# Second attention: the output product without its identity and bias products

## Chip, core and metric

One core of a Trainium2 chip runs the whole program. The metric is the time on the device in microseconds, smaller is better. The three runs of the kernel before took 1669.58, 1671.32 and 1675.81 us, median 1671.32.

## The reference

Two transformer layers over 4096 tokens of width 256. Each layer adds attention and a feed-forward part to its input. The change is in the second layer's attention, a gated linear attention by chunks of 128 tokens:

```python
xn = _layernorm(x, axis=-1)
x = x + _L1_attn_ref(xn, ...) + _L1_ffn_ref(xn, ...)

# in _L1_attn_ref: M is the state of a head, 32 x 32
M = M * f_t[..., None, None] + g_t[..., None, None] * scale * (k_t[..., :, None] * v_t[..., None, :])
y_t = jnp.einsum('bhd,bhde->bhe', q_t, M) * o_t[..., None]
...
return jnp.einsum('bld,ed->ble', y, Wout) + bout
```

So every row of the result is x + y Wout^T + bout, and the second feed-forward part, a mixture of eight experts of which each token takes two, is added to that later.

## The kernel before

The program runs in stages: the first attention and routing (to about 400 us), the first experts, then from about 790 us the rest of the first layer's sums with the norms for the second layer (the shared stage), the second attention (880 to 1130 us), and the second experts, which take the rest. All steps of the middle part stand in one list, `plan2`. Every engine walks through it and does its own share of each step; semaphores tie the engines together, and each engine keeps the list's order. The list is written by hand: `BEHIND` puts steps behind the products of the shared stage, `TURN` and `LATE` are the order of one turn of the second attention, and `AMONG` puts single steps between.

The activations lie in SBUF in `ACC`, 32 chunks of 128 tokens by 256. The second attention takes one chunk a turn, 32 turns, in the order `ORDER1` (all eight batches' first chunks, then the second ones). One turn n holds, on TensorE in this order: the value product (`project_val`, line 1753) for chunk n; the query and key product (`project_qk`, line 1741) for chunk n+1; transposes of queries and keys (`turn`, lines 1769 and 1777); the state products and the sums of chunk n-1 (`keys`, `update`, lines 1813, 1822, 1827); sixteen affinity products of chunk n (line 1795); and the output product of chunk n-1 (`project_out`, lines 1836 to 1840).

The output product accumulates in one PSUM region: the identity times the chunk's rows of `ACC` (this adds x), two products with Wout, and a bf16 product of three rows of ones with the bias split in three bf16 parts (`ones3`, `BO3`). ScalarE then copies the region over the chunk's rows in `ACC` (line 1344) and signals `oe_put`.

The other engines in a turn:
- VectorE: state update (line 2353, turns 8 to 23), the decay scan (`decay`, line 2334, 128x1024, both operands in SBUF), rotary products (lines 2314, 2325, 2326), and the weighing of the affinities (`affinity`, line 2341), which signals `w_put`. `project_val` of the next turn waits for `w_put`, since affinities and values share a PSUM bank.
- ScalarE: value scalings (line 1303), copies of the transposes (1310, 1315), of the sums (1321), key scalings (1339), the output copy (1344).
- GpSimd: opening (`open_gates`, lines 1030 and 1036: the gated queries of chunk n+1, on which the transposes of the next turn wait), and in turns 6 to 29 two or three indirect DMAs that scatter routing rows (line 929), in a pattern of three, three, two. In the shared stage it adds sums of 128x1024 (`sums`, line 1001, and `combine`, line 1011), and at one place it splits the bias (`bias_split`).
- SyncE: loads the decays of each turn (line 802), weights of the second experts (788, 848) and stores finished rows, eight chunks at a time (`store_sums`), when `oe_put` has counted them. Before the second experts TensorE waits for all 32 of `oe_put`.

Of the kernel before, what the change touches and what calls it, by code (L numbers as in the profile page):

```python
# [92 lines left out]
def attention_order():  # L93
# [10 lines left out]
    for idx in range(-LEAD, NH + 7):  # L104
# [83 lines left out]
        ("open", 1), ("decay_load", 2)]  # L188
# [43 lines left out]
def second_order():  # L232
# [19 lines left out]
    out += [("rows",)] + [(kind, NT - 1) for kind in ("update", "sums_copy", "project_out", "out_copy")]  # L252
# [47 lines left out]
def build(nc, t, out):  # L300
    ctx = ExitStack()
    with ctx:
# [140 lines left out]
        BO3 = view(carve(128), 128, BF16)  # L443
        ones3 = view(carve(64), 64, BF16)
# [20 lines left out]
        NB1 = view(small + 186, 32)  # L465
        assert pt_at + 2560 + 2048 <= LIMIT - 7680
# [98 lines left out]
        stk_set, v_set = sem("stk_set"), sem("v_set")  # L565
# [11 lines left out]
        b_in, b_cut, b_rows, b_set = sem("b_in"), sem("b_cut"), sem("b_rows"), sem("b_set")  # L577
# [10 lines left out]
        none_set, slot_in, slot_turned, slot_off, slot_put = (sem(n) for n in ("none_set", "slot_in", "slot_turned", "slot_off", "slot_put"))  # L588
# [27 lines left out]
        out_made, oe_put, sums_out = (sem(n) for n in ("out_made", "oe_put", "sums_out"))  # L616
# [28 lines left out]
        def sync(sp):  # L645
# [50 lines left out]
            def maxrow(n):  # L696
                bk, use = banks0["maxrow", n]
                sp.wait_ge(bank[bk], use + 1)
                sp.wait_ge(s_made, 24 * n + 24)
                sp.wait_ge(stk_set, 3)  # L700
# [9 lines left out]
            def clear(p):  # L710
                sp.wait_ge(cst_in, 32)
                sp.wait_ge(none_set, 4)
# [41 lines left out]
            sp.wait_ge(b_cut, 5)  # L754
            sp.wait_ge(b_set, 1)
# [118 lines left out]
        def gpsimd(pool):  # L874
# [5 lines left out]
            for v in Vb:  # L880
                pool.memset(v, 0.0).then_inc(v_set)
            pool.wait_ge(v_set, 2)
            for v in Vb:
                pool.memset(v[:, :, :, 16:17], 1.0).then_inc(v_set)
            pool.wait_ge(v_set, 4)
            for n in range(3):
                if n:
                    pool.wait_ge(stk_set, n)
                pool.memset(STK[n][1][96:99, :, :].rearrange("p j s -> p (j s)").bitcast(F32), ONES2).then_inc(stk_set)
            pool.wait_ge(stk_set, 3)  # L890

            def clear_meta():
                for n, apart in enumerate((128, 0)):
                    pool.memset(unused[n][0:NTILE, :, :], 0.0).then_inc(none_set)
                    pool.wait_ge(none_set, 2 * n + 1)
                    pool.iota(unused[n][0:NTILE, :, 1], [[1, 128]], base=T, channel_multiplier=apart, allow_small_or_imprecise_dtypes=True).then_inc(none_set)
                pool.wait_ge(none_set, 4)
# [11 lines left out]
            def bias_rows():  # L909
                pool.memset(B2S, 0.0).then_inc(b_set)  # L910
                pool.wait_ge(b_in, 32)
                for k in range(3):
                    if k:
                        pool.wait_ge(b_cut, 2 * k)
                    pool.tensor_copy(b3[0:8, k, :], bstage[0:8, :]).then_inc(b_cut)
                    if k < 2:
                        pool.wait_ge(b_cut, 2 * k + 1)
# [120 lines left out]
            def bias_split():  # L1038

                pool.wait_ge(const1_set, 2)  # L1040
                pool.memset(ones3, 0.0).then_inc(const1_set)
                for k in range(3):
                    pool.wait_ge(const1_set, 3 + k)
                    pool.memset(ones3[32 * k:32 * k + 1, :], 1.0).then_inc(const1_set)
                pool.wait_ge(const1_set, 6)
                pool.tensor_copy(BO3, BO).then_inc(const1_set)
                pool.wait_ge(const1_set, 7)
                pool.tensor_tensor(BO, BO, BO3, ALU.subtract).then_inc(const1_set)
                for k in (1, 2):
                    pool.wait_ge(const1_set, 7 + k)  # L1050
                    pool.tensor_copy(BO3[32 * k:32 * k + 32, :], BO[32 * k:32 * k + 32, :]).then_inc(const1_set)
                pool.wait_ge(const1_set, 10)
                pool.tensor_tensor(BO[64:96, :], BO[64:96, :], BO3[64:96, :], ALU.subtract).then_inc(const1_set)
                pool.wait_ge(const1_set, 11)
                pool.tensor_copy(BO3[64:96, :], BO[64:96, :]).then_inc(const1_set)
                pool.wait_ge(const1_set, 12)

            for kind, *a in plan2:
# [6 lines left out]
                elif kind == "const1":  # L1065
                    const1()
                    bias_split()
# [14 lines left out]
        def scalar(act):  # L1082
# [44 lines left out]
            def project_v(b, half):  # L1127
                bk, use = banks0["project_v", b, half]
                act.wait_ge(v_made, 2 * b + half + 1)
                act.wait_ge(v_set, 4)  # L1130
# [255 lines left out]
        def tensor(pe):  # L1386
# [1085 lines left out]
```

## Time and profile before

| | us |
|---|---|
| span of the profiled execution | 1669.4 |
| median of three runs | 1671.32 |
| PE busy | 1569.7 (94%) |
| PE weight loads busy | 1210.1 (72%) |
| DVE busy | 823.6 (49%) |
| ACT busy | 734.2 (44%) |
| POOL busy | 714.7 (43%) |

PE is TensorE, PEld its weight loads, DVE VectorE, ACT ScalarE, POOL GpSimd and SP SyncE. The times are of one execution that the profiler recorded. The chain that ended last is PE for 79% of the span, DVE for 9%, DMA for 4%. The identity product (line 1836) has 32 calls and the bias product (line 1840) too; a float32 product shows as two matmuls. The rows further down are lines of a timeline or of a table of windows. A busy matmul row can hide waits, since matmuls are pipelined and their ends are modelled; the start of an instruction is what the semaphores let through.

### The profile page before, as it was taken

Reading aid. Unit: us, or ns where it says so; the run is one execution under the profiler, and the core shown is the slowest. Engines: PE = TensorE matmul, PEld = TensorE weight load, DVE = VectorE, ACT = ScalarE, POOL = GpSimd, SP = SyncE. Lnnn points to the kernel's source line nnn. Section 1 sums busy time; section 2 is a strip of 40 time slices with the busy share of each in tenths; the row PEclk is TensorE's granted clock in tenths of the full one; section 3 lists DMA queues with packets and bytes.
Section 4 is the critical chain, followed back from the end, with each engine's and each line's share of the span. In section 5 each row is a group of like instructions: output and inputs, shape, how many; then the busy total and the mean of one; then the engine's idle time right before and its main releaser. Section 6 shows DMA issues by size and latency. Waiting matters only on the chain.

```text
span 1669.4 us, 32480 instructions
## 1 busy us (share of the span) xinstructions
PE 1569.7 (94%) x11054; PEld 1210.1 (72%) x11054; DVE 823.6 (49%) x2298; ACT 734.2 (44%) x1923; POOL 714.7 (43%) x815
## 2 busy tenths in 40 slices
PE   6989989999999999999997799988999999999997
PEld 3545445555548999998664567768999999999996
DVE  6867898787812223221477788873221122222220
ACT  4544545555541222222566466644333233333332
POOL 3122336666523555553810467752333333333332
PEclk9989999999999999999999999999999999999999
DMA  8534325534305222222621396466222222222221
GB/s 269 131 103 110 79 70 105 106 91 103 67 17 230 73 70 72 72 70 88 216 103 65 102 221 99 78 123 259 33 38 39 33 39 39 34 37 39 34 38 23
DMA packets 86093, 151.07 MB, mean 90 GB/s; under 512 B 16276, under 2 KB 64272, under 8 KB 82864
## 3 DMA queue, kind: packets, MB, share of 16 engines
q1 hardware_dynamic: 61392, 111.62, 25.3%
q0 software_dynamic: 24544, 37.38, 10.3%
q8 instruction: 96, 1.57, 0.4%
q14 instruction: 61, 0.50, 0.1%
HBM read 104.10 MB, written 44.45 MB: 89 GB/s over the span
## 4 chain that ended last, share of the span: by engine, by line
PE 79%; DVE 9%; DMA 4%; issue 3%; ACT 3%; SPq 1%; POOL 0%; another core or an unknown queue 0%; DVEq 0%; ACTq 0%; POOLq 0%
PE PS L1634 23%; PE PS L1652 22%; PE PS L1491 4%; PE PS L1427 3%; DVE PS L1954 3%; PE PS L1741 3%; PE PS L1476 3%; PE PS L1455 2%; PE PS L1608 2%; PE PS L1562 2%; PE PS L1619 2%; PE PS L1517 2%; PE PS L1437 2%; PE PS L1753 1%; DMA arena<-FD 1%
## 5 line engine op out<-in xcount | busy, mean ns | idle before, releaser
L1634 PEld LDWEIGHTS PS<-arena 128*128 128x128 f32 x3408 | 396.6, 192 | 15.8 <-DVE arena L2174 4.6
L1634 PE MATMUL PS<-arena 128*128 128x128 f32 x3408 | 403.8, 275 | 3.2 <-DVE arena L2174 3.2
L1652 PE MATMUL PS<-arena 128*128 x1704 | 392.4, 379 | 0.0
L1652 PEld LDWEIGHTS PS<-arena 128*128 128x128 f32 x1704 | 311.7, 190 | 40.2 <-issue 0.2
L2174 DVE COPY arena<-PS 128x256 f32<-128x256 f32 x142 | 60.3, 425 | 414.8 <-PE PS L1619 404.2
L1954 DVE CUSTOM_DVE_ANT_0 PS<-PS,arena 128x512 f32<-128x512 f32 (+3 forms) x512 | 235.5, 523 | 46.1 <-PE PS L1455 42.4
L970 POOL DMA_INDIRECT out<-arena x71 | 111.8, 1574 | 313.1 <-ACT arena L1246 292.4
L1236 ACT ACTIVATE arena<-PS,arena 128x128 f32<-128x128 f32 x568 | 162.3, 369 | 137.6 <-PE PS L1634 137.5
L1246 ACT ACTIVATE arena<-PS,arena 128x256 f32<-128x256 f32 x142 | 67.4, 474 | 283.1 <-PE PS L1654 191.3
L903 POOL TENSOR_SCALAR_AFFINE_SELECT arena<-arena 128x256 f32<-128x256 f32 x256 | 100.0, 414 | 207.9 <-ACT arena L1152 207.5
L1152 ACT ACTIVATE arena<-PS 128x512 f32<-128x512 f32 (+1 forms) x256 | 166.3, 704 | 49.9 <-PE PS L1476 40.3
L956 POOL DMA_INDIRECT arena<-XN,arena x142 | 144.4, 1017 | 93.8 <-PE PS L1619 51.9
L929 POOL DMA_INDIRECT SLOT<-arena x128 | 156.1, 1220 | 30.2 <-issue 30.2
L2186 DVE COPY arena<-arena 128x1024 f32 (+1 forms) x142 | 136.7, 963 | 61.7 <-ACT arena L1228 57.9
L963 POOL DMA_INDIRECT SUM<-arena x71 | 70.3, 990 | 111.6 <-ACT arena L1246 105.0
L1455 PE MATMUL PS<-arena 96*128 96x512 bf16 (+3 forms) x512 | 99.8, 307 | 6.0 <-DVE arena L1954 5.8
L1476 PE MATMUL PS<-arena 99*128 99x512 bf16 (+3 forms) x512 | 98.0, 308 | 5.7 <-ACT arena L1152 4.8
L1228 ACT ACTIVATE arena<-PS 128x512 f32<-128x512 f32 x71 | 42.4, 597 | 113.9 <-PE PS L1634 108.4
L1476 PEld LDWEIGHTS PS<-arena 99*128 99x128 bf16 x512 | 45.6, 99 | 57.8 <-issue 20.2
L1455 PEld LDWEIGHTS PS<-arena 96*128 96x128 bf16 x512 | 49.2, 99 | 46.6 <-DVE arena L1954 16.3
L1491 PE MATMUL PS<-arena 128*32 128x512 f32 (+3 forms) x1024 | 75.7, 435 | 4.5 <-DVE arena L1940 3.6
L2334 DVE TENSOR_TENSOR_SCAN arena<-arena 128x1024 f32<-128x1024 f32 x32 | 73.1, 2286 | 7.6 <-DMA arena<-FD 7.5
(246 smaller groups left out, 1985.6 us busy)
## 6 DMA issues: line engine op xcount, KB each, us to landing
arena<-FD SPq DMA_DIRECT2D x32, 512.0 KB
arena<-in_w SPq DMA_DIRECT2D x16, 1024.0 KB
SPL<-arena SPq DMA_DIRECT2D x32, 384.0 KB, 2.6
arena<-SPL SPq DMA_DIRECT2D x64, 192.0 KB
XN<-arena SPq DMA_DIRECT2D x16, 512.0 KB, 3.2
arena<-SPL SPq DMA_DIRECT2D x64, 128.0 KB
arena<-SUM SPq DMA_DIRECT2D x16, 512.0 KB, 6.4
arena<-in_x SPq DMA_DIRECT2D x8, 512.0 KB, 6.4
```

The lines of the kernel that those rows point to most:

```text
L929: pool.indirect_dma_start(SLOT[layer], bass.IndirectOffsetOnAxis(ap=POS[:, n, i:i + 1], axis=0), META[:, i, n, :], None).then_inc(row_out[ ...
L956: pool.indirect_dma_start(MOE[layer].xr[i % 4][:, :], None, XN, row).then_inc(tile_in[i % 4], 16)
L970: pool.indirect_dma_start(out, row, m.y[i % 3][:, :], None, compute_op=ALU.add).then_inc(y_out[i % 3], 16)
L1152: act.activation(PB[h % NPB][:, lo:hi], ps(3, lo, hi), ACT.Exp, scale=0.25).then_inc(p_made)
L1236: ins = act.activation(m.hT[i % len(m.hT)][:, 128 * f:128 * f + 128], ps(m.UPB[i % 2], 128 * f, 128 * f + 128), ACT.Gelu, bias=m.bias[i % ...
L1455: ins = pe.matmul(ps(0, o, o + w), q[0:96, j, 128 * i:128 * i + 128], k[0:96, j, 0:w], start=True, stop=True)
L1476: ins = pe.matmul(ps(3, o, o + w), k[0:99, j, 128 * kb:128 * kb + 128], q[0:99, j, 128 * kb:512], start=True, stop=True)
L1491: ins = pe.matmul(PS[32 * j:32 * j + 32, 6, 128 * kb:512], vb[:, kb, 8 * half + jj, :], PB[(8 * n + jj) % NPB][:, OFFT[kb]:OFFT[kb] + w], ...
L1634: ins = pe.matmul(o, m.now[i % 2][:, c * F + 128 * f:c * F + 128 * f + 128], m.xt[i % 2][:, 128 * c:128 * c + 128], start=(c == 0), stop=( ...
L1652: ins = pe.matmul(to, m.hT[i % len(m.hT)][:, 128 * c:128 * c + 128], m.WD[:, bass.ds(e * (nf * 256) + c * 256, 256)], start=(c == 0), stop ...
L1954: dve.tensor_tensor_reduce(sc, sc, MASK[:, 384 - 128 * r:512], -1.0, -NEG, ALU.add, ALU.min, NM[n % 2][:, r, j:j + 1]).then_inc(s_max)
L2186: dve.tensor_copy(m.now[i % 2][:, :], m.WU[:, bass.ds(e * m.wrow, m.wrow)]).then_inc(w_staged)
```

## The change

TensorE's output product has only its two products with Wout. ScalarE copies them from PSUM into a single SBUF buffer `OUT1` (over constants that are not read any more) and signals `out_put`. GpSimd adds `OUT1` to the chunk's rows of `ACC` (`out_add`, 128x256) and signals `oe_put`; the step stands behind `open` in a turn, for chunk n-1. ScalarE's copy of chunk n waits for the addition of chunk n-1. The bias is added to `ACC` earlier, 128x1024 for each of the eight batches (`bias_add`), once the second layer's norm of the batch has read them; GpSimd does it at the list's step `xa`. The bias split and its constants are gone, and some semaphores are merged (`stk_set`, `v_set`, `none_set`, `b_set`).

```diff
 TURN = [...
         ("sums_copy", -1), ("project_out", -1), ("keys", 0), ("weigh", 0), ("out_copy", -1), ("rope_add", 1),
-        ("open", 1), ("decay_load", 2)]
+        ("open", 1), ("out_add", -1), ("decay_load", 2)]
...
+        OUT1 = NONE[:, 0:256]
...
-            def bias_split():
...
+            def bias_add(b):
+                pool.wait_ge(xn_made, b + 1)
+                four = ACC[:, 4 * b:4 * b + 4, :]
+                pool.tensor_tensor(four, four, BO.unsqueeze(1).to_broadcast([128, 4, 256]), ALU.add).then_inc(bo_put)
+
+            def out_add(n):
+                i = ORDER1[n]
+                pool.wait_ge(bo_put, min(n + 1, NB))
+                pool.wait_ge(out_put, n + 1)
+                pool.tensor_tensor(ACC[:, i, :], ACC[:, i, :], OUT1, ALU.add).then_inc(oe_put)
...
             def project_out(n):
                 act.wait_ge(out_made, n + 1)
-                act.activation(ACC[:, ORDER1[n], :], ps(1, 256, 512), ACT.Copy).then_inc(oe_put)
+                if n:
+                    act.wait_ge(oe_put, n)
+                act.activation(OUT1, ps(1, 256, 512), ACT.Copy).then_inc(out_put)
...
             def project_out(n):
 
                 if n:
-                    pe.wait_ge(oe_put, n)
-                else:
-                    pe.wait_ge(const1_set, 12)
-                pe.matmul(ps(1, 256, 512), ident, ACC[:, ORDER1[n], :], start=True, stop=False)
+                    pe.wait_ge(out_put, n)
                 pe.wait_ge(yt_put, n + 1)
                 for g in range(2):
-                    pe.matmul(ps(1, 256, 512), YT[:, 128 * g:128 * g + 128], WOUT[:, g, :], start=False, stop=False)
-                pe.matmul(ps(1, 256, 512), ones3[0:96, :], BO3[0:96, :], start=False, stop=True).then_inc(out_made)
+                    ins = pe.matmul(ps(1, 256, 512), YT[:, 128 * g:128 * g + 128], WOUT[:, g, :], start=(g == 0), stop=(g == 1))
+                ins.then_inc(out_made)
```

## Rows read from the trace of the kernel before

**Rows 1.** Windows: start:end, length, busy us of PE, PEld, DVE, ACT, POOL, clock, DMA.

```profile
998.20:1075.70 77.50, 77.50 (x806) 54.61 (x804) 65.17 (x78) 51.78 (x212) 59.36 (x52) 1.00 0.52 91
```

**Rows 2.** Timeline of one turn: start, duration, engine, line, operation, count, idle before.

```profile
1017.15 0.73 PE L1795 MATMUL PS<-arena 32*128 32x128 f32 x16
1017.80 0.70 PE L1836 MATMUL PS<-arena 128*128 128x256 f32 x2
1017.94 1.22 DVE L2341 TENSOR_TENSOR arena<-PS,arena 128x1024 f32<-128x1024 f32 x1 [0.63 <-PE PS L1795]
1018.34 1.03 PE L1839 MATMUL PS<-arena 128*128 128x256 f32 x4
1019.20 0.27 PE L1840 MATMUL PS<-arena 96*128 96x256 bf16 x1
1019.32 1.10 PE L1753 MATMUL PS<-arena 128*128 128x256 f32 x4
...
1021.97 0.60 PE L1769 MATMUL PS<-arena 128*128 128x128 f32 x4
```

**Rows 3.** Timeline: weighing and next value product in two other turns.

```profile
892.90 1.22 DVE L2341 TENSOR_TENSOR arena<-PS,arena 128x1024 f32<-128x1024 f32 x1 [1.05 <-PE PS L1795]
...
894.59 1.03 PE L1753 MATMUL PS<-arena 128*128 128x256 f32 x4
...
1088.38 1.23 DVE L2341 TENSOR_TENSOR arena<-PS,arena 128x1024 f32<-128x1024 f32 x1 [1.06 <-PE PS L1795]
...
1089.75 1.10 PE L1753 MATMUL PS<-arena 128*128 128x256 f32 x4 [0.55 <-DVE arena L2341]
```

**Rows 4.** Timeline of ScalarE in the turn of rows 2.

```profile
1017.34 0.39 ACT L1321 ACTIVATE arena<-PS 128x256 f32<-128x256 f32 x1 [0.91 <-PE PS L1827]
1017.62 1.79 ACT L1339 ACTIVATE arena<-arena 128x32 f32<-128x32 f32 x8
...
1019.51 0.38 ACT L1344 ACTIVATE arena<-PS 128x256 f32<-128x256 f32 x1
```

**Rows 5.** Timeline of GpSimd in that turn, with VectorE's scan.

```profile
1017.40 0.61 POOL L1030 TENSOR_TENSOR arena<-arena 128x256 f32<-128x256 f32 x1 [0.52 <-DVE arena L2326]
1017.97 0.61 POOL L1036 TENSOR_TENSOR arena<-arena 128x256 f32<-128x256 f32 x1
1018.74 1.00 POOL L929 DMA_INDIRECT SLOT<-arena  x1 [0.16 <-issue]
1019.60 2.28 DVE L2334 TENSOR_TENSOR_SCAN arena<-arena 128x1024 f32<-128x1024 f32 x1
1020.05 2.61 POOL L929 DMA_INDIRECT SLOT<-arena  x1 [0.30 <-issue]
...
1022.96 0.96 POOL L929 DMA_INDIRECT SLOT<-arena  x1 [0.30 <-issue]
```

**Rows 6.** Timeline: a GpSimd product that starts within a scan.

```profile
934.99 2.29 DVE L2334 TENSOR_TENSOR_SCAN arena<-arena 128x1024 f32<-128x1024 f32 x1
935.15 2.53 POOL L1030 TENSOR_TENSOR arena<-arena 128x256 f32<-128x256 f32 x1 [10.36 <-DVE arena L2326]
```

**Rows 7.** Timeline: a small VectorE step beside a GpSimd addition.

```profile
806.08 2.35 POOL L1011 TENSOR_TENSOR arena<-arena 128x1024 f32<-128x1024 f32 x1
...
806.84 1.62 DVE L2231 SCALAR_TENSOR_TENSOR arena<-arena 128x4 f32<-128x4 f32 x1
```

**Rows 8.** Timeline of the shared stage's end, ScalarE and VectorE.

```profile
853.52 2.06 ACT L1288 ACTIVATE arena<-arena 128x256 f32<-128x256 f32 x4
...
863.24 0.29 DVE L2255 COPY arena<-PS 128x128 f32<-128x128 f32 x1 [0.72 <-PE PS L1705]
...
865.83 0.16 DVE L2231 SCALAR_TENSOR_TENSOR arena<-arena 128x4 f32<-128x4 f32 x1
```

**Rows 9.** Timeline of the end of the second attention.

```profile
1129.14 0.95 POOL L956 DMA_INDIRECT arena<-XN,arena  x1 [0.30 <-issue]
...
1130.38 0.41 PE L1619 MATMUL PS<-arena 128*128 128x128 f32 x2 [0.52 <-issue]
```

More of the change, by code:

```diff
@@ L251, in second_order @@
             out.append(("slots",))
-    out += [("rows",)] + [(kind, NT - 1) for kind in ("update", "sums_copy", "project_out", "out_copy")]
+    out += [("rows",)] + [(kind, NT - 1) for kind in ("update", "sums_copy", "project_out", "out_copy", "out_add")]
     return out
@@ L587, in build @@
         r_pos = sem("r_pos")
-        none_set, slot_in, slot_turned, slot_off, slot_put = (sem(n) for n in ("none_set", "slot_in", "slot_turned", "slot_off", "slot_put"))
+        slot_in, slot_turned, slot_off, slot_put = (sem(n) for n in ("slot_in", "slot_turned", "slot_off", "slot_put"))
         row_out = [sem(f"row_out{n}") for n in range(4)]
@@ L615, in build @@
         kd_put, y_made, yt_put, dm_made, m_put = (sem(n) for n in ("kd_put", "y_made", "yt_put", "dm_made", "m_put"))
-        out_made, oe_put, sums_out = (sem(n) for n in ("out_made", "oe_put", "sums_out"))
+        out_made, bo_put, oe_put, sums_out = (sem(n) for n in ("out_made", "bo_put", "oe_put", "sums_out"))
+        out_put = sem("out_put")
         xt_ready = {b: [(banks0[f"xt{c}", b][0], banks0[f"xt{c}", b][1] + 1) for c in range(2)] for b in range(NB)}
@@ L699, in maxrow @@
                 sp.wait_ge(s_made, 24 * n + 24)
-                sp.wait_ge(stk_set, 3)
+                sp.wait_ge(pads_set, 7)
                 if n >= 3:
@@ L711, in clear @@
                 sp.wait_ge(cst_in, 32)
-                sp.wait_ge(none_set, 4)
+                sp.wait_ge(const_set, 7)
                 if p == 0:
@@ L880, in gpsimd @@
             for v in Vb:
-                pool.memset(v, 0.0).then_inc(v_set)
-            pool.wait_ge(v_set, 2)
+                pool.memset(v, 0.0).then_inc(pads_set)
+            pool.wait_ge(pads_set, 2)
             for v in Vb:
-                pool.memset(v[:, :, :, 16:17], 1.0).then_inc(v_set)
-            pool.wait_ge(v_set, 4)
+                pool.memset(v[:, :, :, 16:17], 1.0).then_inc(pads_set)
+            pool.wait_ge(pads_set, 4)
             for n in range(3):
                 if n:
-                    pool.wait_ge(stk_set, n)
-                pool.memset(STK[n][1][96:99, :, :].rearrange("p j s -> p (j s)").bitcast(F32), ONES2).then_inc(stk_set)
-            pool.wait_ge(stk_set, 3)
+                    pool.wait_ge(pads_set, 4 + n)
+                pool.memset(STK[n][1][96:99, :, :].rearrange("p j s -> p (j s)").bitcast(F32), ONES2).then_inc(pads_set)
+            pool.wait_ge(pads_set, 7)
             def clear_meta():
                 for n, apart in enumerate((128, 0)):
[L894 to L897, printed above, removed]
+                    pool.memset(unused[n][0:NTILE, :, :], 0.0).then_inc(const_set)
+                    pool.wait_ge(const_set, 2 * n + 4)
+                    pool.iota(unused[n][0:NTILE, :, 1], [[1, 128]], base=T, channel_multiplier=apart, allow_small_or_imprecise_dtypes=True).then_inc(const_set)
+                pool.wait_ge(const_set, 7)
             def future(h):
@@ L1066, in gpsimd @@
                     const1()
-                    bias_split()
+                elif kind == "xa":
+                    bias_add(*a)
+                elif kind == "out_add":
+                    out_add(*a)
                 elif kind == "gates" and a[1] == 4:
```

34 lines of the change are left out of this document (7 added, 27 removed).

## Prediction

> **What bounds the kernel now.** I read the stretch by windows first, then the timeline of one turn, then the list of waits. The second attention runs 32 turns of about 7.05 us. In the eleven turns from 998.2 to 1075.7 us the matmul row is busy for all 77.50 us, and weight loads for 54.61 [rows 1]. That looks like an engine without a gap, so that any product taken out comes back as time. The timeline of one turn says otherwise. The sixteen affinity products start at 1017.15 and end at 1017.88; VectorE's weighing of them (line 2341) starts at 1017.94. TensorE meanwhile runs the identity, output and bias products (1017.80, 1018.34, 1019.20), and the next turn's first value product (line 1753) starts at 1019.32, 1.38 us after the weighing began [rows 2]. Line 1753 waits for the weighing (project_val, w_put). In a turn where TensorE stood idle, with 0.55 us put down to the weighing, it starts at 1089.75, 1.37 us after a weighing that began at 1088.38 [rows 3]. So the distance in the full turn is the distance of a pure wait. I compared all 31 turns that have a next one: in 27 of them the weight load of line 1753 stands 1.33 to 1.35 us behind the start of the weighing. The two limits coincide: TensorE is through with the three products at 1019.20 + 0.11 = 1019.31, and the wait lets it go on at 1017.94 + 1.37 = 1019.31. The loop that sets the turn is value, query and key products, turns, update, affinity, weighing, and value again. The output product lies beside it, under the weighing.
>
> The Trainium skill (Perfetto Trace Analysis, Identifying the Most-Contended Engine) calls matmul busy share a bad measure of headroom and takes the weight-load share instead. By that measure TensorE has a quarter to spare here (54.61 of 77.50), which speaks against the first rival below.
>
> **The change, part by part.**
>
> 1. TensorE loses the identity product (1018.34 - 1017.80 = 0.54 us up to the next, of which 0.11 is behind the affinity products, so 0.43) and the bias product (1019.31 - 1019.20 = 0.11): 0.54 us a turn [rows 2]. What is late next is the weighing, and it is just as late as before: 0 in 27 turns. The identity product also covered the wait for ScalarE's copy of the sums: that copy runs 1017.34 to 1017.73 [rows 4], and the output products can start at 1017.88, so this wait is over by 0.15 us. If it were not, there are 0.54 us before it would show. In two of the four others something is won. After the weighing of 892.90 the value product starts at 894.59, 1.69 us behind it [rows 3], which is 0.3 more than the wait; a second turn is alike, and the last two wait for routing. I take -0.6 us for the stage, between 0 and -1.
>
> 2. ScalarE's copy has the same size and another target. It starts at 1019.51 now, after the key scalings (1017.62, 1.79 us, so to 1019.41) [rows 4]. The products end 0.54 earlier but the scalings don't, so the copy starts no earlier than about 1019.35 and its result is there at about 1019.8. It now waits for the addition of the row before, a turn back; behind it in ScalarE's queue are the next value scalings. GpSimd would have to be over 6 us late. Cost 0. SyncE's stores of eight rows now wait for GpSimd; behind them are the decay loads, but each store comes more than a turn after its last row. Cost 0, except at the end.
>
> 3. GpSimd gains 32 additions of 128x256, placed behind opening (open). The nearest row is its own 128x256 product at 0.61 us [rows 5]. In a turn with three scatters GpSimd idles for 0.52 us only: opening 1.19, scatters 1.00, 2.61 and 0.96 with their gaps. Of three turns two have three scatters and one has two. The second scatter takes 2.61 instead of 0.96 since VectorE's scan (1019.60, 2.28 us) is running [rows 5]. In the turn at 935.15 a 0.61 us product that starts 0.16 us into a scan takes 2.53 [rows 6]. The addition can't start before 1019.8, so GpSimd stands idle from 1018.58 for 1.2 us and then meets the scan 0.2 us after its start: 2.5 us. In exchange no scatter meets it: -1.65. A turn on time thus costs GpSimd 1.2 + 2.5 - 1.65 = 2.1 us, against 0.52 of idle time, and opening is 1.5 us late in the next. What waits for opening are the transposes, at 1021.97 for a result that is there at 1018.0 [rows 2, 5]: some 3.5 us of slack, so still nothing is lost. In the turn after, the addition's input has long been there and it costs 0.6. I followed this for ten turns. A three-scatter turn needs 1.19 + 0.6 + 0.16 + 1.0 + 2 x (0.30 + 0.96) = 5.5 us unblocked, a two-scatter turn 4.2, and a scan blocks about 2.0 (2.53 - 0.61 = 1.9 for a product, 1.65 for a scatter well inside). Three turns: 15.2 + 6.0 = 21.2 against 3 x 7.05 = 21.15. GpSimd is just full. The slack takes up most of the swing; where opening's second product falls into the scan it ends some 0.2 us after the transposes want it, at worst 0.8, and where GpSimd is first the scan starts up to 0.6 later, which VectorE's idle time mostly takes. For the 24 turns with scatters I take 0.1 us a turn, +2.4, between 0 and +8 (0.33 a turn).
>
> 4. In turns 0 to 5 GpSimd has room, but VectorE is on the path with routing steps that read two SBUF operands. Such an operation waits for a GpSimd addition: line 2231, 0.16 us otherwise, took 1.62 beside a 2.35 us addition [rows 7, 8]. Two of the six additions fall on such steps: +0.8, between 0 and +2.
>
> 5. Eight bias additions of 128x1024, 2.35 us each by the same form [rows 7], 19 us in all, go between GpSimd's sums, where it has gaps; the removed bias split was there too. Their own time costs 0. Their blocking does not: the one for batch 5 waits for a norm that ends at 853.52 + 2.06 = 855.6, and holds up the two-operand step that VectorE has just then (line 2293), with all behind it, by some 2.0 us. VectorE has 0.7 us of idle time before 863.24 [rows 8], from which on it is the chain up to 878. So about +1.3; the one for batch 6 comes on that chain, where it delays a step that now another GpSimd sum delays: about -0.1. +1.2 in all, between -0.5 and +5 (two such collisions in full).
>
> 6. The end. TensorE's last stage waits for the last addition instead of the last copy. GpSimd is gathering until 1130.09, then adds for 0.61, and TensorE, which started at 1130.38, starts at about 1130.9 [rows 9]. The products before end earlier, which doesn't help. +0.5, between 0 and +1.
>
> Sum: -0.6 + 2.4 + 0.8 + 1.2 + 0.5 = +4.3 us. The profiled execution has 1669.4; 1669.4 + 4.3 = 1673.7. The median of the runs is 1671.3, 1.9 above it, so I say 1675.6 for a median.
>
> The rule that speaks against the change is in the Trainium skill (SBUF — State Buffer, Who interferes with whom): a VectorE operation with two SBUF inputs and a GpSimd operation that reads SBUF exclude each other, and whichever started first holds the port for its whole length. The trace agrees [rows 6, 7], though the blocked product took 2.53 and not the 2.12 + 0.61 = 2.73 us that full exclusion gives. With 2.73 each meeting would cost 0.2 more, the three turns 21.8 us, and the sum +5 us or so higher.
>
> **The rivals.**
>
> Faster: TensorE's products set the turn, and the coincidence of the two limits is one of the way matmul ends are modelled. For it: the busy row without a gap. Against it: 1.37 us in turns with idle time, 1.38 in those without. 31 x 0.54 = 16.7 us: 1671.3 - 16.7 = 1654.6.
>
> Slower by GpSimd: it becomes the bound of the turns with scatters. For it: 0.52 us idle against 0.6 of new work, and the addition placed just where the scan starts. It decides once opening ends more than 3.5 us later than now. Then the transposes wait in two of three turns for between 0.2 us and the 1.9 by which a blocked product outlasts a free one, say 1.0: 24 x 2/3 x 1.0 = +16 in place of +2.4, so 1689; with half of that 1681.
>
> Slower in the setup: three bias additions hold VectorE up in full, 3 x 2.35 = +7 instead of +1.2: 1675.6 + 5.8 = 1681. Against it: from 812 to 863 the chain is TensorE's almost alone, and VectorE carries it only from 863.24 on [rows 8].
>
> **How the numbers follow.** Forecast 0.60, faster rival 0.10, GpSimd rival 0.19, setup rival 0.11. The ends of the forecast's terms add up to -1.5 and +16, 1669.8 to 1687.3 for a median; all at one end at once is unlikely, and the runs of before lie 6 us apart, so its own range is 1668 to 1683. With the setup rival and most of the GpSimd one, and a little below for the spread, 1665 to 1688 should hold 8 in 10. The line between same and different is 0.5% (8.4 us), about what a measurement of this kernel can tell from no change: 1663 and 1679.7. Faster: the first rival, 0.10. Slower: most of the GpSimd rival (0.16), a third of the setup rival (0.04) and the forecast's tail (0.02), 0.22. Same: 0.68.
>
> **What would show it.** In the changed kernel line 1753 should still start 1.37 us after the weighing, with about half a microsecond of idle time before it put down to VectorE; the turn should stay at 7.05 to 7.2 us; the additions should show two lengths, about 0.6 and about 2.5 us; GpSimd's idle time in the stretch with scatters should be mostly gone. If turns are 6.5 us the first reason is wrong. If transposes (line 1769) wait for GpSimd by a microsecond or more, the second rival holds.

## The result and the profile after

The changed kernel took 1712.3 us (median of four runs, 1706.5 to 1720.9) where the kernel before took 1670.6 beside it: 1.0239 times as long, 95% interval 1.0215 to 1.0263. The forecast was 1675.6 with a range of 1665 to 1688. It was wrong, by 37 us.

The profiled execution has 1709.3 us, 39.9 more than before. Line numbers of the kernel after are 5 to 8 lower than before (value product 1748, transposes 1764, affinity 1790, sums 1822, output product 1831, weighing 2333, scan 2326, scatters 928, addition 1046). From the timelines I took the start of the first value product, of the seventh (turn 6, where the scatters begin), of the last one, and of the first product of the experts:

| us | before | after | difference |
|---|---|---|---|
| first value product at | 874.75 | 875.92 | +1.2 |
| turns 0 to 5 | 58.95 | 60.89 | +1.9 |
| turns 6 to the last value product | 187.51 | 216.44 | +28.9 |
| from there to the experts' first product | 9.18 | 14.06 | +4.9 |
| from there to the end | 539.05 | 541.96 | +2.9 |

Nearly all is in the 25 turns with scatters. The windows of this stretch, before and then after (columns as in rows 1):

```profile
933.70:1121.21 187.51, 177.97 (x1716) 122.93 (x1716) 144.57 (x162) 109.66 (x445) 128.11 (x114) 0.98 0.64 130
```

```profile
936.82:1153.26 216.44, 181.49 (x1641) 122.19 (x1641) 144.88 (x162) 108.23 (x445) 149.69 (x140) 0.93 0.53 112
```

VectorE and ScalarE do the same work in it (144.9 and 108.2 us busy), and GpSimd's 149.7 is far from 216.4. No engine is full; the turn has become longer by waits. The steady turns were 7.05 us and are now 7.7 to 9.9. One with three scatters, which answers to [rows 2, 4, 5]:

```profile
1027.14 2.28 DVE L2326 TENSOR_TENSOR_SCAN arena<-arena 128x1024 f32<-128x1024 f32 x1
1027.20 0.36 ACT L1339 ACTIVATE arena<-PS 128x256 f32<-128x256 f32 x1
1027.71 2.24 POOL L1046 TENSOR_TENSOR arena<-arena 128x256 f32<-128x256 f32 x1 [1.87 <-ACT arena L1339]
...
1029.51 0.60 PE L1764 MATMUL PS<-arena 128*128 128x128 f32 x4
...
1030.10 1.00 POOL L928 DMA_INDIRECT SLOT<-arena  x1 [0.16 <-PE PS L1764]
...
1031.16 0.64 PE L1822 MATMUL PS<-arena 128*32 128x128 f32 x16
1031.41 0.99 POOL L928 DMA_INDIRECT SLOT<-arena  x1 [0.30 <-issue]
...
1031.73 0.89 PE L1790 MATMUL PS<-arena 32*128 32x128 f32 x15
1032.70 0.96 POOL L928 DMA_INDIRECT SLOT<-arena  x1 [0.30 <-issue]
1032.86 0.36 PE L1790 MATMUL PS<-arena 32*128 32x128 f32 x1 [0.24 <-issue]
...
1034.41 0.38 ACT L1314 ACTIVATE arena<-PS 128x256 f32<-128x256 f32 x1 [3.40 <-remote]
1034.57 1.22 DVE L2333 TENSOR_TENSOR arena<-PS,arena 128x1024 f32<-128x1024 f32 x1 [2.68 <-PE PS L1790]
...
1034.94 1.10 PE L1831 MATMUL PS<-arena 128*128 128x256 f32 x4 [1.72 <-ACT arena L1314]
...
1035.94 0.89 PE L1748 MATMUL PS<-arena 128*128 128x256 f32 x3
```

The value product began at 1026.85, and up to the start of the affinity products all stands where it stood: the transposes 2.66 us in (2.65 in [rows 2]), the sums' products at 4.31. These end at 1031.80 by their record. ScalarE's copy of them (line 1314) should follow 0.1 us later; it starts at 1034.41. The weighing, which waits for the affinity products, starts at 1034.57, and the next value product 1.37 us behind it. The trace also has the events that raise the semaphores: the signal of the sums' products comes 2.59 us after the end of their record. In this stretch the signals of three groups come late, each of them sixteen small products on tiles of 32 rows or columns (keys, sums, affinity); those of value, query and key, and output products and of the transposes come 0.01 to 0.02 us behind, in each turn of this trace, also in the middle of a scatter. (In six of the later traces one or two output products come 0.4 to 2.0 us late too, beside a scatter or gather or right behind late affinity products.) Late signals come where scatters run, and those of the sums and the affinities mostly arrive 0.4 to 0.9 us after a scatter has ended (here the last one ends at 1033.66 and the copy starts 0.75 behind). Before the change the last scatter ended 0.3 us before the sums' products did.

I call these signals late, but TensorE itself is held up too. In each turn of the ten traces below that have no late signals, the last of the sixteen affinity products starts 0.46 us behind the first. Here it starts 1.13 us behind (1031.73 and 1032.86), and 17 of the 32 turns of this trace are stretched in this way, to between 0.6 and 1.35 us.

TensorE's clock adds to it. After such a wait it is granted less for a while. Windows of two turns, the second starting right behind a wait of 2.25 us for the copy:

```profile
1000.73:1009.74 9.01, 6.76 (x71) 4.64 (x71) 5.92 (x8) 4.74 (x21) 6.29 (x6) 1.00 0.75 189
1009.74:1019.08 9.34, 8.94 (x72) 5.70 (x71) 5.93 (x8) 4.95 (x22) 6.25 (x6) 0.82 0.36 64
```

In the second the transposes start 4.35 us into the turn, 1.7 later than usual, and the clock over the turn is a mean of its two levels, 2.4 and 1.2 GHz. Over turns 6 on the clock fell from 0.98 to 0.93: (0.07 x 216.4) - (0.02 x 187.5) = about 11 us of full-speed work not granted, an estimate from above of the clock's share in the 28.9. No run separates the two; a kernel below, with additions that nobody reads, had 0.96 over the same turns and they took 219.1 us.

Read with this in mind, the trace of before has it too, in the few turns where scatters met those products (the affinity products, 0.73 us in [rows 2], take 1.28 here):

```profile
946.22 0.62 PE L1827 MATMUL PS<-arena 128*32 128x128 f32 x16
946.83 1.28 PE L1795 MATMUL PS<-arena 32*128 32x128 f32 x16
946.88 0.97 POOL L929 DMA_INDIRECT SLOT<-arena  x1 [0.30 <-issue]
948.15 0.96 POOL L929 DMA_INDIRECT SLOT<-arena  x1 [0.31 <-issue]
949.92 0.39 ACT L1321 ACTIVATE arena<-PS 128x256 f32<-128x256 f32 x1 [3.15 <-remote]
```

The end of the stage answers to [rows 9]:

```profile
1160.10 1.45 POOL L1046 TENSOR_TENSOR arena<-arena 128x256 f32<-128x256 f32 x1 [7.44 <-ACT arena L1339]
1161.69 1.01 POOL L955 DMA_INDIRECT arena<-XN,arena  x1 [0.15 <-issue]
...
1165.52 0.95 POOL L955 DMA_INDIRECT arena<-XN,arena  x1 [0.30 <-issue]
1166.48 0.73 POOL L1046 TENSOR_TENSOR arena<-arena 128x256 f32<-128x256 f32 x1
...
1167.31 0.66 PE L1614 MATMUL PS<-arena 128*128 128x128 f32 x2 [5.07 <-POOL arena L1046]
```

The gathers stand behind the last but one addition, which waits for ScalarE's copy, and the last addition stands behind four gathers.

### The profile page after: what moved, and what is told of

Read it like the earlier page. It is cut to its first block and busy times, and to the rows that moved or that the text cites. A ratio compares the mean times of both kernels' runs of the same rounds, so it can differ in the third digit from the quotient of the medians.

```text
span 1709.3 us, 32410 instructions
## 1 busy us (share of the span) xinstructions
PE 1575.7 (92%) x10958; PEld 1212.5 (71%) x10958; DVE 827.1 (48%) x2298; ACT 731.8 (43%) x1923; POOL 753.5 (44%) x845
## 5 line engine op out<-in xcount | busy, mean ns | idle before, releaser
L1647 PEld LDWEIGHTS PS<-arena 128*128 128x128 f32 x1704 | 312.1, 190 | 39.9 <-issue 0.2
L928 POOL DMA_INDIRECT SLOT<-arena x128 | 130.3, 1018 | 30.2 <-issue 29.3
```

The source lines that it names most:

```text
L928: pool.indirect_dma_start(SLOT[layer], bass.IndirectOffsetOnAxis(ap=POS[:, n, i:i + 1], axis=0), META[:, i, n, :], None).then_inc(row_out[ ...
L1647: ins = pe.matmul(to, m.hT[i % len(m.hT)][:, 128 * c:128 * c + 128], m.WD[:, bass.ds(e * (nf * 256) + c * 256, 256)], start=(c == 0), stop ...
```

## The experiments

The runs came in five groups, each on one chip with the kernel before beside them. The time of the kernel before differs by group (1664 to 1676), so ratios are to its runs in the same one. "Turns 6 on" is the time from the seventh to the last value product. Whether signals came late turned out to go by group:

- group 1: TensorE's half alone, additions that nobody reads, scatters held, additions behind the scatters: on time;
- group 2: the changed kernel, the kernel before, the gathers first, no scatters: late;
- group 3: the changed kernel, additions that nobody reads, scatters held: late;
- group 4: plain transfers by GpSimd and by SyncE, additions behind the scatters, the kernel before with its scatters later: on time;
- group 5: additions behind the scatters, plain transfers by GpSimd, the changed kernel: late.

A kernel without scatters shows no late signals itself, so for it the group is known from the others.

### TensorE's half alone

```diff
-                pe.matmul(ps(1, 256, 512), ident, ACC[:, ORDER1[n], :], start=True, stop=False)
...
-                pe.matmul(ps(1, 256, 512), ones3[0:96, :], BO3[0:96, :], start=False, stop=True).then_inc(out_made)
+                ins.then_inc(out_made)
```

> The kernel before without the identity and the bias product; ScalarE copies the output products alone, so x and the output bias are left out of the result; nothing is added on GpSimd. The step of the forecast that puts TensorE's 0.54 us a turn under the weighing expects no gain: 1671 +- 2. If TensorE's products set the turn: 1655. Theory C (TensorE) expects the slowdown here: 1700 or more.

1664.9 us, 1.0008 times (0.9985 to 1.0031). Turns of 7.05. The products that go leave an idle time of the kind forecast ahead of the value product; VectorE's weighing, then TensorE:

```profile
1000.46 1.23 DVE L2340 TENSOR_TENSOR arena<-PS,arena 128x1024 f32<-128x1024 f32 x1 [0.63 <-PE PS L1795]
```

```profile
1001.83 1.10 PE L1753 MATMUL PS<-arena 128*128 128x256 f32 x4 [0.38 <-DVE arena L2340]
```

The value product starts 1.37 us behind the weighing, with 0.38 us of waiting put down to it. Removing 0.54 us a turn from TensorE is worth nothing, and it costs nothing.

### GpSimd's half alone, and the scatters' place alone

A copy of the addition in the kernel before, with scratch as its target; and no addition, only the wait.

```diff
-        ("open", 1), ("decay_load", 2)]
+        ("open", 1), ("spare", -1), ("decay_load", 2)]
...
+            def spare(n):
+                if n > NT - 5:
+                    return
+                pool.wait_ge(oe_put, n + 1)
+                if n:
+                    pool.wait_ge(spare_put, n)
+                pool.tensor_tensor(SPARE, SPARE, BO, ALU.add).then_inc(spare_put)
```

```diff
+        ("open", 1), ("hold", -1), ("decay_load", 2)]
...
+                elif kind == "hold":
+                    pool.wait_ge(oe_put, a[0] + 1)
```

> The kernel before, its identity and bias products kept, with 28 more additions of 128x256 on GpSimd, each behind opening and waiting for ScalarE's copy as in the changed kernel; nothing reads their result. Theory A (place): the scatters are pushed as in the changed kernel, turns of 7.6 to 9.9 us, time 1671 + 25 to 35 = 1696 to 1706. Theory C (TensorE: the products that were removed kept TensorE's order or its clock in shape, and the slowdown comes from their absence): 1671 to 1674.

> The kernel before with one wait more and no work more: the scatters of a turn wait for ScalarE's copy of the output products of the turn before. They then start about 1.2 us later and the first of three meets VectorE's scan, so the last ends about 1.1 us later than before the change and 1 us earlier than in the changed kernel. Theory A (place) expects a slowdown without any added work, a part of the changed kernel's: 1680 to 1700. Theory B (load): no more work on GpSimd than before, 1671 to 1674.

1.0036 times (1.0015 to 1.0058) and 1.0015 (0.9996 to 1.0033): now each of the three theories had missed in one of the four kernels of this group, A (the scatters' place) in these two, B (GpSimd's load) in the reordered one further down, C (the missing products) in TensorE's half. A turn of the first:

```profile
998.21 1.01 POOL L931 DMA_INDIRECT SLOT<-arena  x1 [0.16 <-issue]
...
999.25 0.64 PE L1839 MATMUL PS<-arena 128*32 128x128 f32 x16
999.52 0.98 POOL L931 DMA_INDIRECT SLOT<-arena  x1 [0.30 <-issue]
...
999.96 0.38 ACT L1333 ACTIVATE arena<-PS 128x256 f32<-128x256 f32 x1 [0.85 <-PE PS L1839]
1000.62 1.23 DVE L2353 TENSOR_TENSOR arena<-PS,arena 128x1024 f32<-128x1024 f32 x1 [0.63 <-PE PS L1807]
1000.80 0.96 POOL L931 DMA_INDIRECT SLOT<-arena  x1 [0.30 <-issue]
```

The scatters do stand where they stand in the changed kernel, and the copy follows the sums' products at once. (On time is not quite zero here: some signals beside scatters are up to 0.27 us behind.) Place alone is not enough. But the changed kernel itself had not run on this chip, so I ran it and the kernel before again.

> The changed kernel once more, unaltered. In the kernel before with additions that nobody reads, the scatters stood just where they stand in the changed kernel (from 1.70 us before to 1.86 us behind the end of the sums' products), and TensorE's signals came 0.04 us behind them, not 2.5 us; so a scatter in that place does not suffice. Theory D (the chip or the execution decides, not the kernel: signals come late on one and not on another): on a chip where the kernel before shows no late signals, this one shows none either, and it is 1664 + 2 to 12. Theory E (the program decides: something in the changed kernel itself, besides the scatters' place, makes the signals late): 1705 to 1720 again, with the lag of 1.2 to 2.6 us in each turn with scatters.

> The kernel before once more, unaltered, for a trace from the same chip. Its first trace has signals of the key products 0.43 us late in turns with three scatters, and 1 to 3 us late in five turns. Theory D: on this chip 0.05 us all through where the changed kernel has the same, and about 1664. Theory E: the same lags as in its first trace, 1670.

1.0225 times (1.0174 to 1.0277) for the changed kernel, with signals up to 2.6 us late; 1.0012 (0.9988 to 1.0036) for the kernel before; the latter had its key products' signals 0.4 us late where the chip of the first experiments showed 0.05 for scatters in the same place. So it could be the chip or the program. The same two kernels once more, beside the changed one:

> The changed kernel a third time, beside two kernels whose signals were on time when they ran. On the chip that ran the four first experiments (chip 5) the kernel before took 1664; on the one that ran the next four (chip 0) it took 1673 and both kernels had late signals. Theory D (the chip decides whether a scatter beside the tiled products makes their signals late): this run and the two others of this call agree: either all show lags of 1 to 3 us and this one is 1.02 times the kernel before, or none does and it is 1.003 to 1.008 times. Theory E (the changed program decides): 1.02 times and lags here, and none in the two others.

> The kernel before with 28 additions more on GpSimd that wait for ScalarE's copy, again. Theory D: on a chip with late signals the scatters that they push cost as much as in the changed kernel, 1.015 to 1.023 times the kernel before; on one without, 1.004 times as the first time. Theory E: 1.004 times and signals 0.05 us behind, whatever the changed kernel does beside it.

> The kernel before with the scatters held until ScalarE's copy and no work more, again. Theory D: on a chip with late signals 1.005 to 1.015 times the kernel before (the last of three scatters lies around 0.0 to 1.0 us behind the sums' products, where the changed kernel's lie up to 1.9); on one without, 1.0015 times as the first time. Theory E: 1.0015 times either way.

1.0221 (1.0186 to 1.0255), 1.0183 (1.0151 to 1.0215) and 1.0073 (1.0050 to 1.0095). The additions that nobody reads, 1.0036 on the first chip, cost 1.0183 here, with the same scatters in the same place:

```profile
998.39 1.00 POOL L931 DMA_INDIRECT SLOT<-arena  x1 [0.15 <-issue]
...
999.46 0.64 PE L1839 MATMUL PS<-arena 128*32 128x128 f32 x16
999.70 1.00 POOL L931 DMA_INDIRECT SLOT<-arena  x1 [0.30 <-issue]
...
1001.00 0.96 POOL L931 DMA_INDIRECT SLOT<-arena  x1 [0.30 <-issue]
...
1002.78 0.38 ACT L1333 ACTIVATE arena<-PS 128x256 f32<-128x256 f32 x1 [3.47 <-remote]
1002.94 1.23 DVE L2353 TENSOR_TENSOR arena<-PS,arena 128x1024 f32<-128x1024 f32 x1 [2.75 <-PE PS L1807]
```

The sums' products end at 1000.10, the copy starts 2.68 us later, against 0.07 above (999.89 to 999.96). Two things are needed together: a scatter beside the small products, and a condition, not identified, in which their signals are late. Given that condition, GpSimd's additions make 1.8 of the 2.2%, and a wait without any work makes 0.7%. The condition belongs to the group of runs: it held for the traces of before and after and for groups 2 and 3, and not for group 1.

### The additions behind the scatters

```diff
-TURN = [("state", -2), ("route", 0), ("project_val", 0), ...
+TURN = [("state", -2), ("route", 0), ("out_add", -2), ("project_val", 0), ...
-        ("open", 1), ("out_add", -1), ("decay_load", 2)]
+        ("open", 1), ("decay_load", 2)]
...
-    out += [("rows",)] + ...
+    out += [("rows",), ("out_add", NT - 2)] + ...
```

> The changed kernel with each GpSimd addition moved behind the scatters of the next turn, and the gathers of the experts ahead of the last two additions. All work is kept. Theory A (place): the changed kernel is slow because the addition, which waits for ScalarE's copy and then for VectorE's scan, pushes the scatters on to TensorE's small tiled products, whose results are then signalled 1 to 3 us late. Here the scatters stand again where they stood before the change, so the turns go back to 7.05 to 7.2 us and the time to about 1712 - 32 (turns) - 3 (end) = 1677, between 1673 and 1683. Theory B (load): GpSimd has too much work in three turns (32 additions of 0.6 us or more); it is as much here, so the time stays above 1700.

1678.1 us, 1.0079 times (1.0051 to 1.0107), as forecast in microseconds; but in the group with signals on time, where that proves little. Twice more, and the changed kernel beside the second:

> The changed kernel with each addition behind the scatters of the next turn and the gathers ahead of the last two additions, again, to have it on a chip with late signals. If the scatters' place is what the changed kernel lost by there: turns of 7.05 to 7.2 us in the steady part, signals of the sums 0.1 us behind, and 1.003 to 1.010 times the kernel before (1.0079 on chip 5). If additions in any place make signals late there: 1.015 or more.

> The changed kernel with each addition behind the scatters of the next turn and the gathers ahead of the last two additions, a third time: both times before, the signals of the tiled products were on time. Its own trace shows in which state the chip is (key products beside a scatter that ends 0.34 us before the sums' end: 0.05 us behind, or 0.4). Late state: if the scatters' place is what the changed kernel loses by, steady turns of 7.05 to 7.2 us and 1.005 to 1.012 times the kernel before, against 1.022 for the changed kernel beside it; if additions in any place cost the same, 1.015 or more. On time: 1.006 to 1.008 as before.

> The changed kernel once more. Late state: 1.022 times, as three times before. On time (never seen for this kernel): if the late signals are the whole of the missed 30 us, turns of 7.05 to 7.2 us in the steady part, and 1.003 to 1.008 times the kernel before, which is what the forecast's own terms give (+4.3) and up to 5 us for the end; if the changed kernel is slow for another reason as well, 1.012 or more.

The first of these had signals on time again, 1.0060 times (1.0037 to 1.0083). The second and third ran together with late signals: 1686.5 us, 1.0056 times (1.0035 to 1.0076), against 1710.2, 1.0198 times (1.0170 to 1.0227), for the changed kernel. Work, operands and engines are the same in both; the order on GpSimd is worth 24 us (turns 6 on: 191.1 us against 216.9). A turn of the reordered kernel, with late signals (the keys' come 0.44 us late in turns with three scatters):

```profile
1018.45 1.00 POOL L928 DMA_INDIRECT SLOT<-arena  x1 [0.15 <-issue]
1019.75 1.90 POOL L928 DMA_INDIRECT SLOT<-arena  x1 [0.30 <-issue]
1021.67 0.74 POOL L1046 TENSOR_TENSOR arena<-arena 128x256 f32<-128x256 f32 x1
...
1022.61 0.64 PE L1822 MATMUL PS<-arena 128*32 128x128 f32 x16
...
1023.32 0.38 ACT L1314 ACTIVATE arena<-PS 128x256 f32<-128x256 f32 x1 [0.85 <-PE PS L1822]
```

The scatters are over before the sums' products begin. Of three steady turns one has 7.05 us and two have 7.15.

### What in a scatter does it

Without the second layer's scatters; with plain transfers of the same bytes by GpSimd; with the same by SyncE.

```diff
...
                 elif kind == "scatter":
-                    scatter(1, *a)
+                    pass
```

```diff
                 for n in picks:
+                    if layer == 1:
+                        pool.dma_start(PLAIN[:, i, n, :], META[:, i, n, :]).then_inc(row_out[r], 16)
+                    else:
...
```

> The changed kernel without the 64 scatters of the second routing; the table of slots stays empty, so the experts work on rows of zeros. Their order of transfers and the routing's other steps are kept. It is read by the stage of the turns alone. Any theory in which scatters, in whatever place, make the signals late: no lag above 0.1 us in any turn, turns of 7.05 us or less, and the last value product 242 to 248 us behind the first. If the lag stays without scatters, the cause is not the scatters but the additions on GpSimd.

> The changed kernel with its 64 second-layer scatters replaced by plain transfers of the same bytes (128 partitions x 2 elements), issued by GpSimd in the same places; the table of slots stays empty, so the experts work on rows of zeros and only the stage of the turns is read. Asks what in a scatter holds TensorE's signals back. If it is GpSimd's issuing of a transfer or the small writes: lags of 1 to 2.6 us as in the changed kernel on the same chip, turns of 7.6 to 9.9 us. If it is the indirection (indices read by GpSimd, one descriptor for each): no lag, turns of 7.05 us. On a chip whose signals are on time for all kernels of this call it tells nothing.

> The same plain transfers, issued by SyncE behind the same addition, with nothing issued on GpSimd in their place; the table of slots stays empty again. If the small writes themselves hold the signals back: lags of about 1 us or more in turns of the stage. If it is GpSimd's part in a transfer: no lag above 0.1 us from them and turns of 7.05 to 7.2 us.

> The changed kernel with plain transfers of the same bytes, issued by GpSimd, in place of the second-layer scatters (slots stay empty, so the experts work on rows of zeros). Late state: lags of 0.5 us and more and turns above 7.1 us if GpSimd's issuing of any transfer holds the signals back; 0.05 us and turns of 7.05 if it takes the indirection. On time: 1.0005 times as before, which tells nothing.

Without scatters, in the group that had the changed kernel at 1.0225: no signal over 0.05 us late, turns of 7.05, and turns 6 on last 175.5 us against 217.3. The last value product comes 236.7 us behind the first, even less than the 242 to 248 expected. So the additions alone, without scatters, delay nothing. The plain transfers and SyncE's fell in a group with signals on time (1.0005 and 0.9998 times), which tells nothing. The fourth run had late signals (the changed kernel beside it 1.0198): 0.9971 times (0.9955 to 0.9987), and again 175.4 us and no late signal.

```profile
1019.42 1.64 POOL L930 DMA_DIRECT2D PLAIN<-arena  x3
...
1020.70 0.64 PE L1826 MATMUL PS<-arena 128*32 128x128 f32 x16
...
1021.41 0.38 ACT L1318 ACTIVATE arena<-PS 128x256 f32<-128x256 f32 x1 [0.85 <-PE PS L1826]
```

GpSimd issues three transfers in 1.64 us; they begin beside the keys' products and end at 1021.06, where the sums' products are half done. In turns 6 to 8 they even end 0.1 to 1.1 us behind the sums' products, and those signals are on time as well. A transfer of GpSimd doesn't hold signals back by being one; the indirect form does. Whether by its length (0.96 to 1.0 us each against 0.55) or by something else in it wasn't separated.

### The gathers ahead of the last additions

```diff
+ ... and not (kind == "out_add" and n == NT - 1):
...
-    out += [("rows",)] + ...
+    out += [("rows",), ("out_add", NT - 2)] + ...
```

> The changed kernel with the gathers of the experts ahead of the last two additions; all work is kept. In the changed kernel the gathers wait behind the last but one addition, which waits for ScalarE's copy, and the last addition behind four gathers. Expected: about 3 us off the end of the changed kernel on the same chip (from the last value product to the first product of the experts 11 us in place of 14), whatever the turns do.

A miss: 1710.4 against 1713.4 us, which the intervals do not separate (1.0215 and 1.0225 times), and from the last value product to the experts 13.05 us against 13.20. What the order could win went to the same effect, since a gather is an indirect transfer too:

```profile
1158.43 0.73 PE L1790 MATMUL PS<-arena 32*128 32x128 f32 x16
...
1160.55 0.94 POOL L955 DMA_INDIRECT arena<-XN,arena  x1 [0.31 <-issue]
1161.51 1.23 DVE L2333 TENSOR_TENSOR arena<-PS,arena 128x1024 f32<-128x1024 f32 x1 [4.59 <-remote]
```

The affinity products end at 1159.16 and the weighing waits until 1161.51, just behind the last gather.

### The kernel before with its scatters later

```diff
-                for _ in range(0 if n < 3 else 2 if n < 6 else 3 if n % 3 else 2):
+                for _ in range(0 if n < 3 else 2 if n < 6 else 0 if n < 9 else 3):
```

> The kernel before with no scatter in the three turns that follow routing (where they lie from 1.3 us before to 2.3 us behind the sums' products and cost it about 6 us on chips 0 and 3), and three in each turn from the tenth on in place of three, three, two. If the place of scatters is the cause there as well: 3 to 6 us faster than the kernel before on a chip with late signals, unless the third scatter of the turns that had two makes GpSimd late (then within 2 us of it); no difference on a chip without.

1.0013 times (0.9986 to 1.0040), with signals on time, where no difference was expected. Whether it helps with late ones stays open.

## Why the prediction was wrong

**TensorE's products (0 gain).** Right. In the changed kernel the value product still starts 1.36 or 1.37 us behind the weighing in 23 of 31 turns, and the run of TensorE's half alone gives 1.0008. (The room by weight loads, 54.61 of 77.50 busy, was nearer three tenths than the quarter I wrote.)

**ScalarE's copy (0).** Right in the turns: 0.36 us, and its wait for the addition never ends last.

**GpSimd's additions (+2.4, at most +8).** This is the step that failed, by some 26 us. What it says of GpSimd alone came out in the kernel with the additions nobody reads and signals on time: additions of 0.7 and of 2.4 to 2.8 us, opening up to 2.2 us nearer to the transposes in the steady turns, and these still 2.65 us into the turn. In the changed kernel the longer turns gave GpSimd room again. Each addition of turns 9 to 25 stands idle for the copy, meets the scan and takes 1.4 to 2.6 us (2.24 above); opening isn't late, and GpSimd idles for 67 us of turns 6 on (59 before), where the forecast had its idle time mostly gone. The Trainium skill's rule (SBUF — State Buffer, Who interferes with whom) that the scan and GpSimd's access exclude each other is borne out here by that 2.24 against 0.72 unblocked. What I left out is what the shift does to others. I wrote that in exchange no scatter meets the scan, and counted it as 1.65 us won. But the blocked scatter of [rows 5] ended 0.8 us behind the scan, still ahead of the sums' products, and the three unblocked ones start 3.8, 3.8 and 2.2 us later in the turn than before (3.25, 4.56 and 5.85 us in), on top of the three groups of small products. That move was put at nothing; it costs 24 us where signals are late, as the reordered kernel shows. I had asked which engine would be late and who waits for GpSimd, and nobody waits for a scatter. The second rival had the place (GpSimd, the addition at the scan) and the wrong mechanism: no transpose waits longer for GpSimd than before.

With signals on time the term was not badly sized. Turns 6 on took 186.4 us with the additional work and 183.8 with TensorE's half alone, on one chip: +2.6, though the kernel with the scatters held, which does no more work than before, had 181.4 there, so single traces differ by as much.

The evidence was in the trace of before. The wait of 3.15 us put down to "remote" above and that of the turn behind it go with two turns of 9.4 and 9.5 us, which are 6.7 and 7.1 in the traces of TensorE's half alone and of the scatters held, with signals on time. I compared the distance from weighing to value product in all turns, found 1.37 in 27 of them, and took the long turns for routing. The distance from the sums' products to their copy would have shown it.

**Early turns (+0.8) and setup (+1.2).** The setup came out about as told: the bias addition for batch 5 starts 0.28 us before a VectorE step of 0.29 us, which then takes 2.33, and the stage starts 1.17 us later. The step takes 2.33 us in all twelve traces with bias additions. From the norm of batch 5 to the first value product they have 22.1 to 22.2 us, and six of the eight others 21.2 to 21.4, so this stretch explains 0.9. The other two (TensorE's half alone, scatters held) have 22.3 and 22.2 without any bias addition, which no run explains; that the sum met the 1.17 so closely is in part luck.

```profile
855.91 2.46 POOL L1040 TENSOR_TENSOR arena<-arena 128x1024 f32<-128x1024 f32 x1 [7.82 <-ACT arena L1281]
856.19 2.33 DVE L2285 SCALAR_TENSOR_TENSOR arena<-arena 128x128 f32<-128x128 f32 x1
```

The early turns cost +1.9 in this pair of traces, the upper part of 0 to +2; over all traces they lie between 59 and 64 us, so it can't be told more closely.

**The end (+0.5).** Mis-sized: +4.9. I had seen the last addition behind the gathers, but not that the last but one holds the gathers up, by its wait of 7.44 us for ScalarE. Putting the gathers first won nothing while they delayed the weighing.

**Behind it (0).** 2.9 us more in the experts' stage, not forecast. All kernels with the changed scheme have 540.4 to 542.3 us there and those with the old one mostly 539.0 to 539.3, but the kernel with the scatters held has 540.4 and 541.2 with no addition on GpSimd. No run was made for this.

**What stays open.** The changed kernel was never seen with signals on time: its four groups of runs all had them late, and the two groups without it had not. The kernel with the additions nobody reads was seen in both conditions, so the program that is being timed doesn't make the condition. Whether chance put the changed kernel on the late side each time, or whether its runs beside them bring the condition to a whole group, wasn't settled, and the chip's number doesn't decide it (0 appears on both sides). What the condition is, no row shows.

Nor do the traces settle what is held: the product, its write or its signal. The Trainium skill (Perfetto Trace Analysis, Summary: the profiler window per engine type) says that the end of a matmul in the trace is an estimate. The trace agrees: the record of the sums' products is 0.64 us long whether the copy starts 0.07 us behind it (999.25 above) or 2.68 us (999.46). Two numbers narrow it down. The stretched starts of the affinity products show TensorE standing still within a group. And of the 14 turns of the changed kernel's trace in which the sums' signal is over 0.9 us late and the affinities' over 0.3, 11 have the affinities' signal only 0.16 us behind the sums', where it is 0.66 to 0.71 in most turns on time; that speaks for affinity products that had run, nearly all, before the sums' signal was out. No version beat the kernel before.

## What to carry to other kernels

Before work is put in front of a transfer on GpSimd, ask what runs on the other engines at the place to which the transfer moves, not only who waits for it. A short wait put down to "remote", or a distance from a product to its copy that is 2 us longer in some turns than in the others, is a cost already there; find what these turns have in common before changing the order. And run the kernel before and the changed one next to each experiment: the additions that nobody reads cost 0.4% in one group and 1.8% in another, and alone the first number would have cleared the scatters' place.

## What was not expected of the hardware

Sixteen tiled products of 32 rows or columns are signalled 0.04 us after the end of their record when nothing disturbs them. Beside an indirect transfer issued by GpSimd that rises to 0.4 to 3.4 us, in some groups of runs and not in others (there 0.27 at most), and the starts within a group of affinity products stretch from 0.46 to as much as 1.4 us, once 2.6. Value products, query and key products and transposes stay at 0.01 to 0.02; output products do but for seven of them, 0.4 to 2.0 us late, in six traces. Plain transfers of the same bytes (0.55 us each) don't do it. In the runs with late signals the kernel before spends 187.5 to 192.9 us in turns 6 on; the changed one without scatters needs 175.5.
